# Expert block weights moved from an indirect gather on GpSimd to register-addressed loads on SyncE, with the first expert bias on TensorE and the hidden split taken from PSUM

## The reference, cut to what matters

```python
logits = z @ router_w + router_b            # z = layernorm(x); 8 experts
scores, idx = top_k(logits, 2); gates = softmax(scores)
h = relu(z @ W1[e] + b1[e])                 # 128 -> 512
y = h @ W2[e] + b2[e]                       # 512 -> 128
x = x + 0.5 * sum over the token's two experts of gate * y
```

## Time and profile before

| | us |
|---|---|
| runs of the kernel before | 1553.53, 1554.93, 1559.62; median 1554.93 |
| profiled execution, its own time | 1563.51 |
| its span, first to last instruction | 1561.5 |
| mean granted TensorE clock | 0.836 of full speed |
| PE / DVE / POOL / ACT busy | 1110.2 / 950.8 / 837.5 / 711.8 |

### The profile page before, as it was taken

One profiled execution on the slowest core, in us unless ns is written; L12 is line 12 of the kernel. 1 busy time (PEld: TensorE's weight loads), 2 busy tenths in 40 slices (PEclk: granted clock), 3 DMA queues, 4 the chain that ended last, 5 costly groups with the idle time before them and its releaser, 6 DMA issues.

```text
span 1561.5 us, 22422 instructions
## 1 busy us (share of the span) xinstructions
PE 1110.2 (71%) x7265; PEld 802.5 (51%) x7265; DVE 950.8 (61%) x2549; ACT 711.8 (46%) x1651; POOL 837.5 (54%) x1081
## 2 busy tenths in 40 slices
PE   1066666899957798987788888878995458574263
PEld 1066654655656665655555564545564446552232
DVE  4354554657644755665658574846557867867746
ACT  2154532456734445663354465535553355453141
POOL 1448655556565674662657553467345683545312
PEclk9999877899976879997888888979996679787576
DMA  9867656644456754445354464244323433410000
GB/s 312 294 212 259 199 199 190 210 136 139 147 181 210 237 185 159 132 153 169 123 187 154 140 184 128 66 158 147 114 84 113 131 129 119 165 49 22 14 1 14
DMA packets 88931, 232.82 MB, mean 149 GB/s; under 512 B 15216, under 2 KB 47344, under 8 KB 72432
## 3 DMA queue, kind: packets, MB, share of 16 engines
q0 software_dynamic: 25472, 142.94, 27.8%
q1 hardware_dynamic: 63344, 88.45, 17.8%
HBM read 175.48 MB, written 55.33 MB: 148 GB/s over the span
## 4 chain that ended last, share of the span: by engine, by line
PE 44%; DMA 12%; DVE 12%; POOL 12%; issue 10%; ACT 6%; SPq 4%; POOLq 0%; DVEq 0%; ACTq 0%
PE bank L531 39%; PE bank L543 5%; DMA Qs<-q_scratch 4%; POOL z_scratch L1420 3%; DMA q_scratch<-ab 3%; DVE hlo L971 2%; POOL yg L1452 2%; POOL wt L1434 2%; POOL hhi L1442 2%; DMA P<-in_w 2%; ACT hfull L1262 2%; DMA k_scratch<-ab 1%; SPq L489 1%; SPq L501 1%; DVE sm_m L1031 1%
## 5 line engine op out<-in xcount | busy, mean ns | idle before, releaser
L531 PE MATMUL bank<-hhi,wt 128*128 128x256 f32 x960 | 232.1, 336 | 105.3 <-DVE hlo L971 102.3
L1031 DVE TENSOR_REDUCE sm_m<-bank 128x4 f32<-128x512 f32 x320 | 212.4, 683 | 139.6 <-PE bank L531 139.4
L971 DVE TENSOR_TENSOR hlo<-hfull,hhi 128x512 fp32r<-128x512 f32 x240 | 194.8, 825 | 134.5 <-POOL hhi L1442 134.3
L531 PE MATMUL bank<-zh,wt 128*128 128x256 f32 x1440 | 244.8, 319 | 17.1 <-DVE zh L963 11.2
L1262 ACT ACTIVATE hfull<-bank,wt 128x256 f32<-128x256 f32 x480 | 198.4, 477 | 106.8 <-PE bank L531 103.7
L531 PEld LDWEIGHTS bank<-hhi,wt 128*128 128x128 f32 x960 | 173.1, 222 | 137.0 <-DVE hlo L971 119.7
L531 PEld LDWEIGHTS bank<-zh,wt 128*128 128x128 f32 x1440 | 214.1, 219 | 34.9 <-issue 12.8
L1434 POOL DMA_INDIRECT wt<-w_scratch,ei x120 | 123.8, 1031 | 197.5 <-ACT yb L1270 175.3
L1313 ACT ACTIVATE P<-bank 128x512 f32<-128x512 f32 x320 | 180.8, 601 | 96.4 <-PE bank L531 95.5
L1442 POOL TENSOR_SCALAR hhi<-hfull 128x512 fp32r<-128x512 f32 x240 | 163.0, 687 | 99.4 <-ACT hfull L1262 96.1
L1420 POOL DMA_INDIRECT z_scratch<-zb,pos x128 | 135.5, 1058 | 86.0 <-DVE pos L952 51.6
(11 more groups left out here) (183 smaller groups left out, 1879.5 us busy)
## 6 DMA issues: line engine op xcount, KB each, us to landing
zin<-z_scratch SPq DMA_DIRECT2D x120, 128.0 KB
y_scratch<-yt SPq DMA_DIRECT2D x120, 128.0 KB, 2.7
w_scratch<-wt SPq DMA_DIRECT2D x8, 1024.0 KB, 13.3
q_scratch<-ab SPq DMA_DIRECT2D x32, 256.0 KB, 4.2
k_scratch<-ab SPq DMA_DIRECT2D x32, 256.0 KB, 3.4
Ks<-k_scratch SPq DMA_DIRECT2D x64, 128.0 KB, 3.7
Qs<-q_scratch SPq DMA_DIRECT2D x64, 128.0 KB, 3.9
P<-in_w SPq DMA_DIRECT2D x8, 512.0 KB, 11.3
```

The lines of the kernel that those rows point to most:

```text
L531: return e.matmul(o, lhs, rhs, start=start, stop=stop, **kw)
L971: e.tensor_tensor(hlo[s % 4][:, :, :], hfull[s % 3][:, :, :], hhi[s % 4][:, :, :].bitcast(F32), ALU.subtract).then_inc(*d_hid.step(s, "lo"))
L1031: e.tensor_reduce(bn_m[:, k, s_, :], blocks(shared("maxi", i, 0, s_)), AX.X, ALU.max).then_inc(*d_max.step(i, f"m{s_}"))
```

## The change

SP gets the `wload` step: it waits for the same events as POOL did, reads the block's expert number from SBUF into a register, and issues two plain DMAs at addresses computed from it, the 128 rows of 8,200 bytes and, new, 2 rows of 2 KB with b1 split in a high and a low part. b1 no longer rides in the weight rows: a K = 2 matmul (two rows of b1 by two rows of ones) per chunk opens each accumulation of `hid`. ACT writes `hhi` (one activation of 512 columns, relu, rounded) from PSUM; DVE makes `hlo` = max(PSUM, 0) - `hhi` from PSUM. `hfull` and POOL's step are gone. `res` issues its four matmuls with `hhi` first and waits for `hlo` only before the last two. The bank of `hid` is free after DVE's step, where it was free after ACT's. ACT's step now waits for `res` of half s - 4, as POOL's did; it no longer waits for `hlo` of half s - 3. The plan's costs and edges follow, two edges of other stages are corrected, and at the start b1 is loaded and split on DVE.

```diff
-WROW = 2048 + NC + 1
+WROW = 2048 + 2
-    "wload": ("G1.1+6", [], 1),
+    "wload": ("S.3+6", [], 1),
-    "hid": ("P.72 A.85 G.68 D.8", [(0, 1)], 1),
+    "hid": ("P.95 A.6 D.7", [(0, 2)], 1),
...
-              + "P.88<20 A.69 D.75 P.88<20 D.75 " * NF + "P2.6 G1.4<16 D.7<36,37",
+              + "P.88<20 A.69 D.75 P.88<20 D.75 " + "".join(
+                  f"P.88<20 A.69<{20 + 5 * c},{21 + 5 * c} D.75 P.88<20 D.75 " for c in range(1, NF)) + "P2.6 G1.4<16 D.7<36,37",
...
     if stage == "hid":
-        return [[("zin", u // 2, 3), ("wload", u // 2, 0), ("hid", u - 3, 3), ("hid", u - 3, 1)], [], [("res", u - 4, 0)], []][k]
+        return [[("zin", u // 2, 3), ("wload", u // 2, 0)], [("res", u - 4, 0)], []][k]
...
     if stage == "scor":
-        if k == 0:
-            return [("mrow", u // 5, 3)]
-        return [("val", (u - PR // 2) // 5, (0, 0, 1, 1, 2)[(u - PR // 2) % 5])] if k < 3 else []
+        ring = [("val", (u - PR // 2) // 5, (0, 0, 1, 1, 2)[(u - PR // 2) % 5])]
+        return ring + [("mrow", u // 5, 3)] if k == 0 else ring if k < 3 else []
...
# SP, begin(): b1 is loaded behind xs[1], and its two parts stored to b_scratch
+                e.dma_start(ob[0:NE, :], a["b1"]).then_inc(l_first, 16)
...
+                w.wait_ge(*d_init.at(0, "b1"))
+                for i, part in enumerate((mr[:, :].bitcast(F32), flat(hd)[0:NE])):
+                    e.dma_start(bd.rearrange("(e i) c -> e i c", i=2)[:, i, :], part).then_inc(s_bias, 16)
...
# SP, new stage (it goes from POOL)
+            def wload(u):
+                f, k = divmod(u, KB)
+                w.wait_ge(*d_route.at(f, "ei"))
+                if u == 0:
+                    w.wait_ge(s_bias, 48)
+                    for n in range(WR):
+                        w.wait_ge(s_w[n], 16 * (NE // WR))
+                if u >= WR:
+                    w.wait_ge(*t_res.at(2 * (u - WR) + 1, "y"))
+                    w.wait_ge(*a_yout.at(u - WR, "y"))
+                row = e.value_load(ei[0:1, f % 2, k:k + 1], min_val=0, max_val=NE - 1)
+                e.dma_start(wt[u % WR][:, :].bitcast(F32), wd[bass.DynSlice(row * 128, 128), :]).then_inc(l_wt[u % WR], 16)
+                at = 32 * (u % WR)
+                e.dma_start(wb[at:at + 2, :].bitcast(F32), bd[bass.DynSlice(row * 2, 2), :]).then_inc(l_wt[u % WR], 16)
...
# PE, hid
-                    mm(o[:, c, :], w1[:, 0, cs], z[:, 0, :], c == 0, False, skip_group_check=True)
+                    mm(o[:, c, :], wb[at:at + 2, cs], oner[at:at + 2, :], c == 0, False, skip_group_check=True,
+                       tile_position=(at, 0))
+                    mm(o[:, c, :], w1[:, 0, cs], z[:, 0, :], False, False, skip_group_check=True)
...
# PE, res
-                w.wait_ge(*d_hid.at(s, "lo"))
+                w.wait_ge(*a_hid.at(s, "hi"))
...
-                for c in range(2):
-                    cs = slice(128 * (2 * (s % 2) + c), 128 * (2 * (s % 2) + c) + 128)
+                cols = [slice(128 * (2 * (s % 2) + c), 128 * (2 * (s % 2) + c) + 128) for c in range(2)]
+                for c, cs in enumerate(cols):
                     mm(o, w2[:, 0, cs], hhi[s % 4][:, c, :], s % 2 == 0 and c == 0, False)
                     mm(o, w2[:, 1, cs], hhi[s % 4][:, c, :], False, False)
+                w.wait_ge(*d_hid.at(s, "lo"))
+                for c, cs in enumerate(cols):
                     t = mm(o, w2[:, 0, cs], hlo[s % 4][:, c, :], False, s % 2 == 1 and c == 1)
...
# DVE, begin
+                e.memset(oner[:, :].bitcast(F32), 1.0)
+                e.tensor_copy(mr[:, :], ob[0:NE, :]).then_inc(*d_init.step(0, "b1h"))
+                w.wait_ge(*d_init.at(0, "b1h"))
+                e.tensor_tensor(flat(hd)[0:NE].bitcast(F32R), ob[0:NE, :], mr[:, :].bitcast(F32), ALU.subtract
+                                ).then_inc(*d_init.step(0, "b1"))
...
# DVE, route: one operation less
-                then(e.tensor_scalar(fl, fl, 7.0, 128.0, ALU.min, ALU.mult), "k3")
-                e.tensor_scalar(ei[:, f % 2, :], fl, part, None, ALU.add).then_inc(*g.step(f, "ei"))
+                e.tensor_scalar(ei[:, f % 2, :], fl, 7.0, None, ALU.min).then_inc(*g.step(f, "ei"))
...
# DVE, hid
-                e.tensor_tensor(hlo[s % 4][:, :, :], hfull[s % 3][:, :, :], hhi[s % 4][:, :, :].bitcast(F32), ALU.subtract
-                                ).then_inc(*d_hid.step(s, "lo"))
+                e.scalar_tensor_tensor(out=hlo[s % 4][:, :, :].rearrange("p c t -> p (c t)"), in0=shared("hid", s, 0), scalar=0.0,
+                                       in1=hhi[s % 4][:, :, :].rearrange("p c t -> p (c t)").bitcast(F32), op0=ALU.max,
+                                       op1=ALU.subtract).then_inc(*d_hid.step(s, "lo"))
...
# ACT, hid
-                b1 = wt[u % WR][:, 2048:2048 + NC].bitcast(F32)
-                o = shared("hid", s, 0).rearrange("p (c t) -> p c t", c=2)
-                for c in range(2):
-                    k = 2 * (s % 2) + c
-                    t = e.activation(hfull[s % 3][:, c, :], o[:, c, :], ACT.Relu, bias=b1[:, k:k + 1])
+                if s >= 4:
+                    w.wait_ge(*t_res.at(s - 4, "y"))
+                e.activation(hhi[s % 4][:, :, :].rearrange("p c t -> p (c t)"), shared("hid", s, 0), ACT.Relu
+                             ).then_inc(*a_hid.step(s, "hi"))
...
# POOL, hid: gone, as is wload
-                e.tensor_scalar(hhi[s % 4][:, :, :], hfull[s % 3][:, :, :], 1.0, 0.0, ALU.mult, ALU.add).then_inc(*p_hid.step(s, "hi"))
```

More of the change, by code:

```diff
@@ L105, in follows @@
     if stage == "hid":
[L106 removed]
+        return [[("zin", u // 2, 3), ("wload", u // 2, 0)], [("res", u - 4, 0)], []][k]
     if stage == "res":
[L108 removed]
+        return [("hid", u, 2)] + ([("yout", u // 2 - 1, 0)] if u % 2 == 0 else [])
     if stage == "yout":
@@ L270, in build @@
         zh = [sb(f"zh{i}", [128, 2, SB], F32R) for i in range(2)]
-        hfull = [sb(f"hfull{i}", [128, 2, SB]) for i in range(3)]
+        wb = sb("wb", [128, 512], F32R)
+        oner = sb("oner", [128, SB], F32R)
         hhi = [sb(f"hhi{i}", [128, 2, SB], F32R) for i in range(4)]
@@ L301, in build @@
         slots, kth, part = small[:, 45:49], small[:, 49:49 + KB], small[:, 64:65]
-        go_on, bt = small[:, 65:65 + 8 * TILES], small[:, 193:233].rearrange("p (e c) -> p e c", e=NE)
+        go_on, bt = small[:, 65:65 + 8 * TILES], small[:, 193:193 + 2 * NE].rearrange("p (e c) -> p e c", e=NE)
         biasb = small[:, 233:361]
@@ L319, in build @@
         wd = nc.dram_tensor("w_scratch", [NE * 128, WROW], F32, kind="Internal").ap()
+        bd = nc.dram_tensor("b_scratch", [NE * 2, 512], F32, kind="Internal").ap()
         zd = [nc.dram_tensor(f"z_scratch{i}", [SLOTS, D], F32, kind="Internal").ap() for i in range(2)]
@@ L336, in build @@
         s_out = sem("s_out")
-        d_init, p_init = flow("d_init", "identb half mask tri bank keys"), flow("p_init", "zero clear")
+        d_init, p_init = flow("d_init", "identb half b1h b1 mask tri bank keys"), flow("p_init", "zero clear")
         a_split, d_split = flow("a_split", "hi"), flow("d_split", "lo")
@@ L520, in sync_program @@
             begin()
-            follow("S", {"sload": sload, "split": split, "zin": zin, "yout": yout, "proj": proj, "stack": stack, "mrow": mrow,
+            follow("S", {"sload": sload, "split": split, "wload": wload, "zin": zin, "yout": yout, "proj": proj, "stack": stack, "mrow": mrow,
                          "mxb": mxb})
@@ L1269, in yout @@
                     w.wait_ge(*t_yout.at(u - 2, "t"))
-                e.activation(yb[u % 2][:, :], y_bank[:, 0:SB], ACT.Identity, bias=wt[u % WR][:, WROW - 1:WROW].bitcast(F32)
+                e.activation(yb[u % 2][:, :], y_bank[:, 0:SB], ACT.Identity, bias=wt[u % WR][:, 2048:2049].bitcast(F32)
                              ).then_inc(*a_yout.step(u, "y"))
@@ L1421, in scat @@
                                          zb[:, i // 4, i % 4, :], None).then_inc(s_slot[f % 2], 16)
-                yield
-            def wload(u):
-                f, k = divmod(u, KB)
-                w.wait_ge(*d_route.at(f, "ei"))
-                if u == 0:
-                    w.wait_ge(s_bias, 16)
-                    for n in range(WR):
-                        w.wait_ge(s_w[n], 16 * (NE // WR))
-                if u >= WR:
-                    w.wait_ge(*t_res.at(2 * (u - WR) + 1, "y"))
-                    w.wait_ge(*a_yout.at(u - WR, "y"))
-                e.indirect_dma_start(wt[u % WR][:, :].bitcast(F32), None, wd,
-                                     bass.IndirectOffsetOnAxis(ap=ei[:, f % 2, k:k + 1], axis=0)).then_inc(l_wt[u % WR], 16)
-                yield
-            def hid(s):
-                w.wait_ge(*a_hid.at(s, "h"))
-                if s >= 4:
-                    w.wait_ge(*t_res.at(s - 4, "y"))
-                e.tensor_scalar(hhi[s % 4][:, :, :], hfull[s % 3][:, :, :], 1.0, 0.0, ALU.mult, ALU.add).then_inc(*p_hid.step(s, "hi"))
                 yield
@@ L1522, in gpsimd_program @@
```

(5 more changed lines are left out.)

28 lines of the change are left out of this document (13 added, 15 removed).

## The result

Three runs of the changed kernel took 1620.43, 1626.11 and 1632.95 us, median 1626.11, against 1554.93 before: a ratio of 1.0445, 95% interval 1.0384 to 1.0506. The change makes the kernel 4.5% slower. The forecast was 1528 us, 27 us faster; the result lies above the whole range of 1478 to 1590.

A forecast was written before the change was run, and what follows sets the result against it. No engine is full: a net of short steps bounds the kernel, PE its largest part. Terms -81 - 8 - 3 + 46 + 14 + 5 = -27 us take the profiled 1563.5 to 1536.5, for the median 1528; range 1478 to 1590.

The forecast's parts named there:

- PE gets 480 matmuls of 256 columns: Added b1 matmuls in `hid`, 0.154 us each: 74 us of PE, 46 us on the chain; PE bounds 51 and 119.
- PE becomes the bound: Rival, chance 0.15: where PE is nearly full, all 74 us of extra matmuls count and only POOL-caused waits return; 1578 us, slower.
- The rest of the sum: All terms except PE's added b1 matmuls: -81, -8, -3, +14 and +5 us.
- The gathers' terms: Weight gathers leave POOL: gains of 31 us on the chain, 5 of issue before them, 3 at the start.
- the DMA queue: SP's transfers stand behind weight loads in one queue: 14 us lost, bounds 0 and 93.
- The hidden stage's terms without the bias: Gains: POOL's rounding 31 us, ACT 9, DVE's subtraction 5, `res` issuing earlier 8; loss: `hid` banks held longer, 5.
- The single steps: Signs in the profile after: POOL near 550 us, `hhi` 0.60, `hlo` 0.69, PE 60 to 80 us busier, `hlo` waits under 60.
- SP's work: Register read 0.5 us and two DMA issues of 0.6 each per block, 204 us of SP, covered by its waiting; nothing added.
- 69 in the rival: Rival, chance 0.12: key and query loads and q stores stand behind 1 MB weight loads in one queue; 1583 us, slower.
- the rival on the clock: Rival, chance 0.18: without PE's long waits the blocks' granted clock rises from 0.85 towards 0.93; 1500 (half) or 1473 us (all).

The follow-up runs named there:

- the 128-row bias: Changed kernel with b1 resident as a 128-row stationary tile, zero but for 16 rows, a selector column as moving operand, no second SP load: 0.9643, median 1514.18 us.
- the kernel with the dearer plan cost: Changed kernel with only the planner's PE price of `hid` raised from 0.95 to 1.75 us: 1.044 times the kernel before (one run, 1622.87 us).
- the hidden stage alone: Kernel before with the new hidden stage, b1 added by 128-row matmuls, and the weight gather still on POOL: 0.9624.
- three versions: Kernel before with weight loads on SP, 0.9603; with new hidden stage and 128-row b1 matmuls, 0.9624; changed kernel with 128-row b1 matmuls, 0.9643.

## Why the prediction was wrong

**The step that failed** is "PE gets 480 matmuls of 256 columns": "No row has two input rows; the nearest are those of `hid`, with 128", from which came 0.125 us, 74 us of PE and 46 on the path, with bounds of 51 and 119. The runs show 0.506 us each in close sequence at full clock and 0.81 at the lower level, 267 us of PE, and 143 us of time. The share of it that I put on the path was near: 143 of 267 us is 54%, where I had 62%. I took rows to be free and columns to be the price, and so bounded the cost within one shape, though the change puts a shape between others. The trace of before had nearer rows. This is its timeline of PE at 306 us, where attention's matmuls of 34 rows stand between those of 128:

```profile
305.56 0.50 PE L531 MATMUL bank<-hhi,wt 128*128 128x256 f32 x2
305.90 0.27 PE L531 MATMUL bank<-hlo,wt 128*128 128x256 f32 x1
306.02 0.40 PE L531 MATMUL bank<-hhi,wt 128*128 128x256 f32 x2
306.26 0.28 PE L531 MATMUL bank<-hlo,wt 128*128 128x256 f32 x1
306.47 0.56 PE L531 MATMUL bank<-Qs,Ks 34*128 34x256 f32 x4
```

From `hlo` to the 34-row matmul it is 306.47 - 306.26 = 0.21 us, where from `hlo` to the full `hhi` it is 0.12. And the first two `hhi` at 305.56, which follow other 34-row matmuls, need 0.34 us to the `hlo` behind them, where the two at 306.02 need 0.24. The medians of the whole trace of before, at full clock, are those of the changed kernel: 0.209 us from `hlo` into the 34-row matmul, and 0.207 from a 34-row one to a full one and 0.224 to the full one behind that. Two changes in each of 480 chunks at 0.19 us, with the matmul's own 0.12, make 0.50 us and 240 us of PE, over three times the term I used.

**The rival "PE becomes the bound"** (0.15) named what happened, and the sign that it gave, PE above 80% with its waits for `hlo` gone and the time not shorter, is what the page shows. Its 1578 us rested on the same 74 us of PE and missed by 48. It turned at 28 us more on the path; the short rows gave about 193 us more PE work than forecast and 97 us more on the path (143 where I had 46). Its condition, that the extra matmuls cost in full, wasn't met over the whole kernel: 143 of their 267 us reached the time.

**The rest of the sum** came to -73 us without the bias, and without the bias matmuls -4.8% is -74. That is a right total over wrong parts. The gathers' terms (31 + 5 + 3, less 14 for the DMA queue) make 25 us, and SP's loads alone (with the plan edges, 0.35% by themselves) gave 4.0%, 62. The hidden stage's terms without the bias (31 + 9 + 5 + 8 - 5) make 48, and alone it gave 3.8%, 58, with some of it spent on the 128-row bias. Shares of the chain were added up as if the parts could not serve each other's gain; either part alone reaches further than its share, and together they give less than their sum.

**The single steps.** Right: POOL 526.9 us busy (forecast 550); `hhi` 0.596 and `hlo` 0.687 us (0.60 and 0.69); waits for `hlo` 16.7 us at L553 and 6.1 at L565 (under 60); the queues 39.1% and 3.3% (42% and 3%). DVE lost 56.1 us where I said 30, of which 194.8 - 163.2 = 31.6 are in `hlo`. PE was 277 us busier where I said 60 to 80. Had the bias been in 128 rows, its term would have been too large, not too small: 31 us of PE and 1.2%, 18 us, where I had 74 and 46. SP's work came out as forecast in total, 1.76 us a block (median, from the start of the register read to the end of the second issue) where the sum had 1.7, but its parts didn't. The read (ns, least, median and most; first and last start in us), then the timeline of the issues:

```profile
L495 SPq TENSOR_LOAD <-ei x120: 433/442/1512, 62.9 to 1438.9; - x120
L495 SPq FUSED_REGOPS  x120: 152/156/183, 63.4 to 1439.4; - x120
...
120.30 0.35 SPq L496 DMA_DIRECT2D wt<-w_scratch  x1
120.84 0.30 SPq L498 DMA_DIRECT2D wb<-b_scratch  x1
121.18 0.33 SPq L474 DMA_DIRECT2D zin<-z_scratch  x1
```

Two issues and what lies between them take 0.84 us, where the sum had 1.2; from the start of the read to the first issue it is 0.91 us (median), where it had 0.5. The read itself is 0.442 us, the register operation behind it 0.156. The cover was there: SP still waits 261.6 us for `yt` and 246.4 for `yb` of block u - 4.

**The DMA queue**, +14 us in the sum and 69 in the rival, shows as no loss: the loads on SP alone made the kernel 4.0% faster. The rule of the Trainium skill on turns between queues, in DMA: Bandwidth & Descriptors, section Queues, rings and completion order, made me expect longer landings behind 1 MB loads in one ring. The traces show shorter ones of the stacked loads (3.9 to 2.7 us) and of q (4.2 to 3.5) and longer ones of k (3.4 to 5.0, though 3.5 in the kernel with the dearer plan cost), and PE's waits for `Qs` fell from 39.3 to 3.7 us, so that case fell. Why most are shorter wasn't tried, and no run has the term's own size.

**The clock** didn't rise with the changed kernel: 0.84 in the blocks' stretch, 0.85 before. Over the whole span it was 0.826, where the kernel before had 0.836. With the loads on SP it was 0.852 and with the hidden stage alone 0.861, which fits a small part of the rival on the clock; but the kernel without bias matmuls, with the best ratio of all, had 0.832 in its profile, so no run shows the clock as the cause of a gain.

## What to carry to other kernels

Price an added matmul by its place, not by its columns: between full ones, one of few rows (2 to 34 here) costs two changes of mode of 0.19 us each. Fill up the rows with zeros (to 128 here; 66 rows went as fast), or put all the short ones side by side. Look for the kind of step in the trace at hand before taking a price from it: this one stood in the trace of before. And before adding work to the engine that is busiest, ask how much of its idle time lies where the work goes: 92 us of PE cost 10 here, and the next 143, at a lower clock as well, cost 115.

When two edits relieve the same queue, test each alone. Here the loads on SP with nothing on PE (0.9603) are the simplest of three versions, 0.9603 to 0.9643, that beat both kernels and can't be told apart.
